# Block 0 of the relation by chunks of the depth, and another order of loads on the sync queue

## The reference

```python
fused    = concatenate([x, x_mean * ones_L, hidden[:, None, :] * ones_L], axis=-1)
relation = relu(einsum('bld,do->blo', fused, W) + b)       # W: 1536 x 512
# quant_linear: activations in uint8 with one scale for the whole tensor (its maximum),
# weights in int8 with one scale per output channel, bias rounded to the product of both
h   = relu(quant_linear(relation, w1, b1))                  # w1: 2048 x 512
out = x + quant_linear(h, w2, b2)                           # w2: 512 x 2048
```

## Time and profile before

| | before |
|---|---|
| median of 3 runs | 348.81 us |
| lowest and highest | 348.67 and 349.97 us |
| the profiled execution | 349.05 us |
| its span, first to last instruction | 346.8 us |
| granted TensorE clock, mean | 1.00 |
| busy: TensorE, VectorE, ScalarE | 97%, 78%, 45% |

### The profile page before, as it was taken

One profiled execution on the slowest core, in us unless ns is written; L12 is line 12 of the kernel. 1 busy time (PEld: TensorE's weight loads), 2 busy tenths in 40 slices (PEclk: granted clock), 3 DMA queues, 4 the chain that ended last, 5 costly groups with the idle time before them and its releaser, 6 DMA issues.

```text
span 346.8 us, 5358 instructions
## 1 busy us (share of the span) xinstructions
PE 337.3 (97%) x1645; PEld 196.2 (57%) x1645; DVE 271.4 (78%) x590; ACT 155.7 (45%) x263; POOL 1.1 (0%) x8
## 2 busy tenths in 40 slices
PE   6999999999999999999999999989999999999996
PEld 5788888888868544444444444434444444444444
DVE  1877668658684789999999999988486595685996
ACT  2635225325412499970000000038959559568800
POOL 1000000000000000000000000000000000000000
PEclk9999999999999999999999999999999999999999
DMA  7965998964432128886781030037984399977116
GB/s 247 404 214 171 325 326 241 285 188 177 121 60 41 21 122 363 346 347 287 323 335 60 0 121 0 0 121 289 402 341 183 133 412 424 361 241 227 78 60 242
DMA packets 29934, 74.90 MB, mean 216 GB/s; under 512 B 17864, under 2 KB 18144, under 8 KB 22496
## 3 DMA queue, kind: packets, MB, share of 16 engines
q1 hardware_dynamic: 29920, 74.73, 59.7%
HBM read 45.37 MB, written 25.17 MB: 203 GB/s over the span
## 4 chain that ended last, share of the span: by engine, by line
PE 90%; DVE 4%; issue 3%; DMA 2%; SPq 0%; ACT 0%; DVEq 0%
PE bank L480 28%; PE bank L436 26%; PE bank L360 25%; PE bank L501 4%; PE bank L348 4%; DMA x_in<-in_x_dram 2%; PE bank L453 1%; DVE hidden L781 1%; DVE x_lo L618 1%; PE bank L448 1%; PE bank L399 1%; DVE steps L842 0%; DVE cw_lo L656 0%; PE bank L418 0%; SPq L225 0%
## 5 line engine op out<-in xcount | busy, mean ns | idle before, releaser
L436 PE MATMUL bank<-pool_r,w_t 128*128 (+1 forms) x480 | 103.8, 379 | 0.0
L781 DVE TENSOR_SCALAR_CACHE_REDUCE hidden<-bank,qb,hmax 128x512 f32 x128 | 97.6, 808 | 5.3 <-DVE hidden L781 1.5
L576 ACT ACTIVATE steps<-hidden,s_quant 128x512 int16 (+1 forms) x124 | 76.8, 708 | 21.1 <-DVE w_t L809 11.2
L436 PEld LDWEIGHTS bank<-pool_r,w_t 128*128 128x128 bf16 x480 | 47.0, 98 | 56.6
L480 PE MATMUL bank<-w_t 128*128 128x512 bf16 x256 | 56.2, 379 | 0.9 <-DVE w_t L844 0.9
L360 PE MATMUL bank<-x_hi,cw_hi 128*128 128x512 f32 x128 | 51.0, 398 | 0.8 <-issue 0.5
L360 PE MATMUL bank<-x_hi,cw_lo 128*128 128x512 f32 x128 | 49.9, 390 | 0.0
L360 PE MATMUL bank<-x_lo,cw_hi 128*128 128x512 f32 x128 | 49.9, 390 | 0.0
L623 DVE TENSOR_SCALAR_CACHE_REDUCE hidden<-bank 128x512 f32 (+1 forms) x31 | 21.3, 689 | 27.9 <-PE bank L360 27.9
L480 PEld LDWEIGHTS bank<-w_t 128*128 128x128 bf16 x256 | 24.8, 98 | 31.7 <-DVE w_t L844 1.5
L480 PE MATMUL bank<-w_t,pool_q 128*128 128x512 bf16 x192 | 41.9, 379 | 0.0
(11 more groups left out here) (101 smaller groups left out, 244.7 us busy)
## 6 DMA issues: line engine op xcount, KB each, us to landing
hidden_spill<-hidden SPq DMA_DIRECT2D x16, 1024.0 KB, 3.9
hidden<-hidden_spill SPq DMA_DIRECT2D x16, 1024.0 KB, 7.7
pool_q<-in_L_ffn_w_dram SPq DMA_DIRECT2D x8, 1024.0 KB, 5.5
pool_r<-in_x_dram SPq DMA_DIRECT2D x8, 1024.0 KB, 5.6
x_in<-in_x_dram SPq DMA_DIRECT2D x7, 1024.0 KB, 5.6
out_dram<-pool_r SPq DMA_DIRECT2D x7, 1024.0 KB, 4.2
pool_r<-in_L_cond_W_dram SPq DMA_DIRECT2D x1, 2048.0 KB, 11.0
x_in<-in_x_dram SPq DMA_DIRECT2D x2, 512.0 KB, 5.4
```

The costliest lines, as they stand in the source:

```text
L436: mm = pe.matmul(bank[ft % BANKS][:, :], w1_t[:, ft, k, :], act_q[:, bass.ds(n * (KD * TB) + k * TB, TB)], start=(k == 0), stop=(k == KD - 1))
L576: ins = act.activation(steps[:, q % 2, f, :], hidden[:, bass.ds(slot * HB + ft * TB, TB)], ACT.Copy, scale=s_quant[:, ft:ft + 1])
L781: dve.tensor_scalar(hidden[:, bass.ds(slot * HB + ft * TB, TB)], bank[ft % BANKS][:, :], qb1[:, ft:ft + 1], hmax[:, ft:ft + 1], ALU.add, A ...
```

## The change

Three things are changed; the operations of phases 2 and 3 are not.

1. **Block 0 goes by chunks of the depth.** Its loads are four, one to each chunk of the depth (runs of 512 bytes), and ScalarE issues the four loads of the relation's weights itself. TensorE turns chunk 0, and then for each chunk makes 4 products hi by hi, 4 lo by hi, turns the next chunk, and makes the 4 products hi by lo. Block 0's four output chunks accumulate at once in banks 4 to 7, and the columns go to bank 3. `turn_x(1)` stands in the last chunk, after the products of output chunk 0. The unused products are 30 and 6.
2. **VectorE's order in block 0.** The column copies stand between chunks 1 and 2. Then come take_relation 0, take_lo of chunk 0 of block 1, take_relation 1, take_lo of chunk 1, and so on to chunk 3, and after these scale_w and cast_w of block 0, one directly behind the other. Block 1 then runs in the old order.
3. **The sync queue.** x's block n + 3 is issued ahead of weight block n + 2. The remaining weights of the relation stand behind turn_w of n = 3, and b2 behind that of n = 5.

```diff
-            load_half(0, x0_landed)
-            load_cw(range(KD // 2))
-            load_half(1, x_landed[0])
+            x_first = x_blocks[0].rearrange("p (j d) -> p j d", d=D)
+            for k in range(KD):
+                sp.dma_start(x_in[:, 0, :, k * P:(k + 1) * P], x_first[:, :, k * P:(k + 1) * P]
+                             ).then_inc(x0_landed[k], 16)
...
-            load_cw(range(KD // 2, KD))
             load_x(1, 1)
             load_w(w1_chunks, 0, 0)
             load_w(w1_chunks, 1, 1)
...
+            sp.wait_ge(x_turned, KD)
+            load_x(2, 0)
+            for n in range(NB):
+                if n + 3 < NB:
+                    sp.wait_ge(x_turned, KD * (n + 2))
+                    load_x(n + 3, (n + 1) % 2)
+                if n + 2 < NB:
+                    sp.wait_ge(w_steps_ready, 4 * (n + 1))
+                    if n + 2 < KD:
+                        load_w(w1_chunks, n + 2, n % 2)
+                    else:
+                        load_w(w2_chunks, n + 2 - KD, n % 2)
+                turn_w(n)
+                if n == 3:
                     sp.dma_start(cw_rest, cw_rows[:, KD:3 * KD, :]).then_inc(rest_landed, 16)
+                if n == 5:
                     sp.dma_start(b2_b[:, :], b2.partition_broadcast(P)).then_inc(b2_landed, 16)
...
+            REL0 = bank[4:8]
+            def turn_x0(k):
+                pe.wait_ge(x0_landed[k], 16)
+                for j in range(TJ):
+                    mm = pe.transpose(XT[k][:, j * P:(j + 1) * P], x_in[:, 0, j, k * P:(k + 1) * P], ident[:, :])
+                mm.then_inc(x_turned, 1)
+            def product0(k, ot, w, v):
+                return pe.matmul(REL0[ot][:, :], w[:, k, ot * P:(ot + 1) * P], v[:, 0, k, :],
+                                 start=(k == 0 and w is cw_hi and v is x_hi),
+                                 stop=(k == KD - 1 and w is cw_lo))
+            keep_warm(30, ident_bf[:, :], bank[4])
+            turn_x0(0)
+            keep_warm(6, ident_bf[:, :], bank[5])
+            for k in range(KD - 1):
+                pe.wait_ge(cw_hi_ready, k + 1)
+                pe.wait_ge(hi_ready, k + 1)
+                for ot in range(KD):
+                    product0(k, ot, cw_hi, x_hi)
+                pe.wait_ge(cw_lo_ready, k + 1)
+                for ot in range(KD):
+                    product0(k, ot, cw_lo, x_hi)
+                if k == 1:
+                    turn_columns()
+                if k + 1 == KD - 1:
+                    pe.wait_ge(cols_taken, 1)
+                turn_x0(k + 1)
+                pe.wait_ge(lo_ready, k + 1)
+                for ot in range(KD):
+                    product0(k, ot, cw_hi, x_lo)
+            k = KD - 1
...
+            for ot in range(KD):
+                product0(k, ot, cw_hi, x_lo)
+                product0(k, ot, cw_lo, x_hi).then_inc(rel_done, 1)
+                if ot == 0:
+                    turn_x(1, 1, 1)
...
-            for k in range(KD // 2):
-                take_cw(k)
-            take_hi(0, 0, range(KD // 2))
-            for k in range(KD // 2, KD):
+            for k in range(KD):
+                act.dma_start(cw_in[:, k, :], cw_rows[:, k, :]).then_inc(cw_landed[k], 16)
+            for k in range(KD):
                 take_cw(k)
                 take_hi(0, 0, [k])
...
-            with dve.Fori(0, KD // 2) as it:
-                for par in range(2):
-                    phase1_block(2 * it + par, it, par, False, False)
+            for ot in range(KD):
+                take_relation(0, ot, bank[4 + ot])
+                take_lo(1, 1, [ot])
+            scale_w(0, 0, 0, False)
+            cast_w(0)
+            for n in range(1, KD):
+                phase1_block(n, n // 2, n % 2, False, False)
```

More of the change, by code:

```diff
@@ L139, in adaln_quantized_ffn @@
         REL = bank[4:6]
-        x0_landed = sem("x0_landed")
+        x0_landed = [sem(f"x0_landed{k}") for k in range(KD)]
         x_landed = [sem("x_landed0"), sem("x_landed1")]
@@ L341, in keep_warm, with turn_x @@
                     pe.matmul(free_bank[:, 0:moving.shape[-1]], ident_bf[:, :], moving, start=True, stop=True)
-            def turn_x(n, it, par):
-                pe.wait_ge(x_landed[par], 16 * (it + 1))
+            def turn_x(n, landed, par):
+                pe.wait_ge(x_landed[par], 16 * landed)
                 for k in range(KD):
@@ new lines, in product0, with turn_columns @@
+            def product0(k, ot, w, v):
+                return pe.matmul(REL0[ot][:, :], w[:, k, ot * P:(ot + 1) * P], v[:, 0, k, :],
+                                 start=(k == 0 and w is cw_hi and v is x_hi),
+                                 stop=(k == KD - 1 and w is cw_lo))
+            def turn_columns():
+                pe.wait_ge(rows_landed, 48)
+                turned = bank[3]
+                for k in range(CK):
+                    pe.transpose(turned[:, k * B:(k + 1) * B], cond_rows[:, k, :], ident[0:B, 0:B])
+                pe.transpose(turned[:, CONDB_AT:CONDB_AT + KD], condb_rows, ident[0:KD, 0:KD])
+                pe.transpose(turned[:, B1_AT:B1_AT + FT], b1_rows, ident[0:FT, 0:FT]).then_inc(cols_turned, 1)
@@ L380, in _ @@
+            k = KD - 1
+            pe.wait_ge(cw_hi_ready, KD)
+            pe.wait_ge(hi_ready, KD)
+            for ot in range(KD):
+                product0(k, ot, cw_hi, x_hi)
+            pe.wait_ge(lo_ready, KD)
+            pe.wait_ge(cw_lo_ready, KD)
+            for ot in range(KD):
[3 more added lines that the diff above has]
+                    turn_x(1, 1, 1)
             with pe.Fori(0, NB // 2 - 1) as it:
-                for par in range(2):
-                    n = 2 * it + par
+                for par in (1, 0):
+                    n = 2 * it + 2 - par
@@ L383, in _ @@
                     relation(n, par, 0)
-                    turn_x(n + 1, it + par, 1 - par)
+                    turn_x(n + 1, it + 2 - par, 1 - par)
                     for ot in range(1, KD):
                         relation(n, par, ot)
[L388 to L392, removed]
             pe.wait_ge(mean_ready, 2)
@@ L657, in take_cw_lo, with take_columns @@
                                   ).then_inc(cw_lo_ready, 1)
[L659 to L662, removed]
+            def take_columns():
+                step(dve.tensor_reduce(fold[:, :], ident[:, :].rearrange("p (g q) -> p q g", q=Q)[:, 0:B, :],
+                                       AX.X, ALU.add))
+                dve.wait_ge(cols_turned, 1)
+                step(dve.memset(rows[:, 0:(KD + CK) * Q], 0.0))
+                step(dve.tensor_copy(bias_in[:, KD:KD + CK, 0:B],
+                                     bank[3][:, 0:CK * B].rearrange("p (k b) -> p k b", k=CK)))
+                step(dve.tensor_copy(condb_col[:, :], bank[3][:, CONDB_AT:CONDB_AT + KD]))
+                dve.tensor_copy(b1_col[:, :], bank[3][:, B1_AT:B1_AT + FT]).then_inc(cols_taken, 1)
+            dve.wait_ge(ident_ready, 1)
+            for k in range(KD):
                 take_cw_lo(k)
                 take_lo(0, 0, [k])
[L666 to L674, removed]
+                if k == 1:
+                    take_columns()
             def phase1_block(n, it, par, w2_rows, last, means=False):
```

26 lines of the change are left out of this document (3 added, 23 removed).

## The result

The changed kernel takes 353.76 us as the median of 4 runs (352.13 to 354.71), against 348.74 before (the median of four runs, one more than in the table above). The ratio is 1.013, with a 95% interval of 1.008 to 1.018: slower by 5.0 us, where 4.4 us were forecast. The profiled execution took 354.71 us against 349.05, and its span 352.5 us against 346.8.

A forecast was written before the change was run, and what follows sets the result against it. TensorE, 97% busy, was taken as the bound. First product 7.8, 14.1 to R, 21.8 to turn_x(3) and 0.4 for the clock give 44.1 against 39.67: +4.4, so 353.2 us, own range 351.9 to 354.5, 8-in-10 range 350.9 to 355.3.

The forecast's parts named there:

- R: Start of take_relation(0, 1), the take of block 0's second finished output chunk; forecast at F + 14.1, or 21.9 us.
- The holes: TensorE idle ahead of relation(1, 0), (1, 2) and (1, 3), waiting for VectorE's takes: 1.4, 1.95 and 2.5, together 5.85 us.
- The first product: Start of TensorE's products in block 0: 7.8 us, between 7.0 and 9.5, against 10.61 before.
- Both bounds: Landing of x's chunk 0, bounded by earlier loads: 5.3 us from below, about 7.6 from above; 6.0 was taken.
- the clock: Block 0's first products run partly at TensorE's lower clock level: a loss of 0 to 0.5 us, taken as 0.4.
- From R to turn_x(3): Stretch through block 1 to the first transposition of turn_x(3), holes included: 21.8 us.
- The sync queue: The new order of loads and turns costs and gains nothing; the nearest cover is 8 us.
- The late first chunk: Rival: chunk 0 of x lands behind the weights at 7.6 or later; +5.6 to +6.4, 354.8 us; chance 0.16.
- The covered hole: Rival: VectorE does not stand still 2.7 us at the cast, the other holes stay; +1.7 us, 350.5; chance 0.09.
- The faster case: Rival: TensorE does not wait for VectorE's queue and the earlier start stays; 346.2 to 347.4 us; chance 0.06.
- the forecast's case without holes: The early start alone, with no TensorE holes: a gain of 1.45 us.
- F: Time of block 0's first product on TensorE: forecast 7.8 us, own range 7.0 to 8.6.

The follow-up runs named there:

- e2_scale_early: The changed kernel with scale_w(0) moved ahead of take_relation(0, 0), the cast left in place; 349.12 us, ratio 0.9999.
- e3_take_between: The changed kernel with take_relation(1, 0) moved between scale_w(0) and cast_w(0); 354.02 us, ratio 1.014.
- e8_turn_early: e7_bank_rule with the next chunk of block 0 turned right behind the four products hi by hi; 346.86 us, ratio 0.994.
- e7_bank_rule: e2_scale_early with relation(1, 0) and relation(1, 1) waiting only for their own bank's take, block 0's third and fourth takes behind take_lo; 347.82 us, ratio 0.9963.
- e4_holes_filled: The changed kernel with 18 and 26 unused products ahead of relation(1, 2) and relation(1, 3); 352.13 us, ratio 1.008.
- e1_sync_queue_alone: The kernel before with only the new order of the sync queue; 348.80 us, ratio 0.999.
- e6: e2_scale_early with the order take 0, lo 0, take 1, take 2, lo 1, lo 2, lo 3, take 3; 348.45 us, ratio 0.998.
- e5_old_order: The changed kernel with VectorE's old order for block 0 too, the start by chunks kept; 353.12 us, ratio 1.011.
- e9: e8_turn_early with 22 unused products at the start instead of 30; 347.01 us, ratio 0.9951.

## Why the prediction was right, step by step

**The mechanism held.** The forecast was that an early start of TensorE would be handed over to VectorE's queue, where the cast stands still behind its scaling, and that TensorE would come to a halt three times. All three halts are there, each released by the take that was named, at R + 1.96, 10.92 and 15.98 against the forecast's R + 1.97, 11.13 and 16.32 (R is 21.89 in the trace). The wait at the cast is 2.63 us against 2.7. The holes are 5.0 us instead of 5.85, since TensorE reached the first two 0.17 us later than reckoned, and the second and third ended 0.2 and 0.3 us earlier: VectorE's steps and hand-overs were a little shorter than priced. Two small readings of the forecast were off: its cast, from 9.11 with 1.22, ends at 10.33 and not at 10.38, and what VectorE did in block 1 before while ScalarE made its steps was three take_lo, one take and the start of a fourth take_lo, not two takes. e2_scale_early shows the cause and not only the pattern: with scale_w(0) ahead, the cast's wait and the two later holes vanish together. e3_take_between shows that it is the length of the queue that counts, for the second hole removed came back in the third but for the 0.6 us of the moved job.

**The first product** was put at 7.8 us and came at 7.01, the lower end. The term that was mis-sized is the landing of x's first chunk, taken as 6.0. The chunk was issued at 0.74 and landed 3.6 us later (DMA issues of the kernel after, the window around the first issues of both queues):

```profile
x_in<-in_x_dram SPq DMA_DIRECT2D x1, 256.0 KB, 3.6
pool_r<-in_L_cond_W_dram ACTq DMA_DIRECT2D x1, 256.0 KB, 2.7
```

So it was there at 4.3, and the 30 idle products, through at 5.1, set the start. Both bounds were too late: they were read off loads with more bytes ahead. The Trainium skill (DMA: Bandwidth & Descriptors, "Queues, rings and completion order") has each DMA engine go round the queues packet by packet. Read as in the prediction, with one run to a packet, it would have brought x's chunk late. The direction is there: the weights' first chunk, of the same size and issued 0.14 us after x's, landed after 2.7 us and not 3.6, and the fourth ones needed 6.5 and 7.2 us. The size is not, since x's first chunk landed 1.7 us before the 6.0 of the forecast. x's fourth chunk was there at 10.0 (2.8 + 7.2), a little later than the 9.6 estimated and still hidden.

**From there to R** the forecast had 14.1 us plus 0.4 for the clock, and the trace has 14.9. The clock cost about what was expected: the first eight products took 2.28 us instead of 1.82, 0.46. The three waits between chunks cost about 0.2 each, where 0.1 was reckoned; e8_turn_early took them away and gained 1.0 us against e7_bank_rule in the medians, 0.9 at turn_x(3). That R came at 21.89, where the forecast had 21.9 without its clock term, is luck: the first product came 0.8 us too early for it, and the way from there took 0.8 us longer.

**From R to turn_x(3)**, 21.8 was forecast and 23.2 measured. The sum had a term for the clock at the start and none behind the holes, so it put a cost at nothing without a reason. The fall of the clock cost 1.6 us in the profiled execution, and two of the four runs have it by their mean clock. e4_holes_filled shows that it hangs on TensorE standing still. The two runs of the changed kernel without it lie 3.4 and 4.1 us over before, the two with it 5.9 and 6.0. The forecast of +4.4 lies between two levels that it didn't know of.

Added up at turn_x(3), the forecast of 44.1 missed 45.07 by 1.0: -0.8 for the first product, +0.4 from there to R, -0.8 for the holes, +1.6 for the clock behind them, and +0.6 for a later end of block 0 (0.17) and the start behind each hole, where twelve products took 2.85 to 2.90 us instead of 2.73. The mechanism was right, and the number is closer than its terms, because their errors partly cancelled.

**The sync queue** was priced at nothing, and e1_sync_queue_alone agrees (ratio 0.999). In the kernel after, TensorE waits for no transfer up to the end of phase 1.

**The rivals.** The late first chunk fell with the landing at 4.3. The covered hole fell with the 2.63 us in the timeline. The faster case was put at 346.2 to 347.4 if VectorE's queue weren't the bound. e6 to e8 took that bound away step by step and came to 348.5, 347.8 and 346.9. The nearest to the forecast's case without holes is e7_bank_rule, 1.3 us under the kernel before. The forecast had 1.45 with its F of 7.8, but 2.65 with F at 7.0 and no loss by the clock, and F was 7.0. The longer waits between the chunks (0.3) and the clock at the start (0.5) took part of the difference. e8_turn_early, which turns the next chunk earlier and so goes beyond the forecast's case, won another 1.0. The change lost because the same edit set VectorE's jobs of block 0 in a bad order.

## What to carry to other kernels

When a stage is made to start or finish earlier, follow what it sets free on the other engines' queues, instruction by instruction, for two blocks further: VectorE was 77% busy and still stopped TensorE three times, two of them through an instruction that waited for ScalarE right behind the one that released ScalarE. Put a job that releases another engine well ahead of the job that waits for it. And when TensorE is left idle for a microsecond or two several times in a row, look at the granted clock behind it, because the halts can cost more than their own length.

## What the runs showed of the hardware that was not expected

- Holes of 1.25, 1.57 and 2.21 us, from 22.6 to 37.9 us, brought TensorE down to 1.2 GHz in two of four runs, a wait of 1.1 and one of 3.2 us (e3_take_between) in four of four, and a single one of 4.1 us (e5_old_order) in four of four; the level lasted 3.4 us in the changed kernel and cost 1.6 us. With a single wait of 1.6 us (e2_scale_early) the mean clock stayed at 0.998 or above in all twelve runs. A mean of 0.998 need not cost anything: in the profiled executions of e6 and e9 it comes from the time after TensorE's last product, where the granted clock falls to 0.50. That halts of different lengths act so is what was seen; the rule behind it can't be read off these runs.
- The page's granted clock does not show the start: it reads full speed while the same product takes 0.63 us instead of 0.39, until 14.6 us in one execution with the old start (e1_sync_queue_alone). In another, that of rows 4, the lower level lasted until 8.9 us, by transpositions of 421 ns instead of 273. In the profiled executions with 30 idle products the engine was at its upper level by 8.5 us each time.
- Of two loads of 256 KB that were issued side by side on two queues, the one in runs of 2 KB landed after 2.7 us and the one in runs of 512 bytes after 3.6; of the fourth pair, after 6.5 and 7.2.
